# Key stacking transfers of items 19 to 23 issued by ScalarE instead of SyncE, in a four-layer attention, expert and depth-routing kernel

## The reference

```python
x = x + L0_xattn(layernorm(x), ctx, mask)    # cross attention, self attention, gelu FFN, 16 heads of 16
x = x + L0_ffn(layernorm(x))                 # 7 experts + no-op, top 2 of 8, capacity 256
x = x + L1_xattn(layernorm(x), ctx, ctx)     # cross attention, 16 heads of 16
x = x + L1_ffn(layernorm(x))                 # upper half of the tokens by score through a gelu FFN
# attention: softmax(q k^T / 4) v, then a projection
```

## Time and profile before

| | us |
|---|---|
| median of 3 runs | 857.49 |
| lowest and highest of them | 852.05, 859.93 |
| the profiled execution | 855.1 |
| its span, first to last instruction | 853.1 |
| mean granted TensorE clock | 0.929 |

### The profile page before, as it was taken

The page is one execution under the profiler, slowest core; times in us unless marked ns, Lnnn a source line. Parts: engine busy times, 40 slices in busy tenths (PEclk is TensorE's granted clock), DMA queues, the critical chain, the costliest instruction groups (busy, mean ns, idle before and its releaser), DMA issues.

```text
span 853.1 us, 18296 instructions
## 1 busy us (share of the span) xinstructions
PE 729.4 (85%) x7218; PEld 607.8 (71%) x7218; DVE 648.7 (76%) x1250; ACT 455.6 (53%) x695; POOL 409.2 (48%) x395
## 2 busy tenths in 40 slices
PE   5788999999999778999894599993677889888897
PEld 4666777777777546999883599992455657656897
DVE  7768888888888653799887377756876889877864
ACT  4256777777777566656432144421145557667342
POOL 7874654534665454624466241107577236473400
PEclk9979999999999899999995699996769989999999
DMA  6687786679776602000030577634586637500011
GB/s 190 131 136 119 140 125 99 104 118 140 115 107 102 88 3 99 26 1 22 24 128 11 154 235 245 194 68 110 86 148 95 98 60 106 85 2 2 13 39 49
DMA packets 57065, 81.47 MB, mean 95 GB/s; under 512 B 8434, under 2 KB 35057, under 8 KB 56932
## 3 DMA queue, kind: packets, MB, share of 16 engines
q1 hardware_dynamic: 53730, 74.11, 45.1%
q0 software_dynamic: 3072, 6.04, 2.9%
q10 hardware_dynamic: 178, 0.16, 0.1%
HBM read 36.74 MB, written 10.11 MB: 55 GB/s over the span
## 4 chain that ended last, share of the span: by engine, by line
PE 61%; DVE 19%; issue 7%; DMA 4%; ACT 4%; POOL 2%; SPq 1%; another core or an unknown queue 0%; ACTq 0%; DVEq 0%; POOLq 0%
PE ps L216 13%; PE ps L218 11%; PE ps L217 11%; PE ps L785 7%; PE ps L853 7%; DVE nmax L1623 6%; PE ps L807 5%; ACT prob L1151 2%; PE ps L827 2%; DMA kst<-k_parts 2%; POOL gat L1469 1%; PE ps L240 1%; PE ps L249 1%; SPq L568 1%; DMA gat<-moe_out,slu 1%
## 5 line engine op out<-in xcount | busy, mean ns | idle before, releaser
L1623 DVE TENSOR_REDUCE nmax<-ps 128x4 f32<-128x1024 f32 x192 | 234.3, 1223 | 69.8 <-PE ps L785 65.0
L1151 ACT ACTIVATE prob<-ps 128x1024 f32<-128x1024 f32 x192 | 196.4, 1023 | 70.4 <-PE ps L807 64.5
L1380 POOL TENSOR_TENSOR rstd<-var,half 128x2 f32<-128x2 f32 x56 | 43.9, 785 | 243.7 <-DVE var L1550 173.0
L785 PE MATMUL ps<-kst,qst 50*128 50x256 f32 (+1 forms) x768 | 99.6, 339 | 34.0 <-DVE nmax L1623 27.3
L853 PE MATMUL ps<-prob,vext 128*32 128x256 f32 x1536 | 107.0, 398 | 1.2 <-ACT oext L1164 1.2
L785 PEld LDWEIGHTS ps<-kst,qst 50*128 50x128 f32 (+1 forms) x768 | 60.9, 196 | 66.0 <-DVE nmax L1623 44.8
L807 PE MATMUL ps<-qst,kst 51*128 51x256 f32 (+1 forms) x768 | 83.3, 296 | 14.6 <-ACT prob L1151 13.8
L807 PEld LDWEIGHTS ps<-qst,kst 51*128 51x128 f32 (+1 forms) x768 | 61.6, 194 | 21.4 <-ACT prob L1151 17.1
L853 PEld LDWEIGHTS ps<-prob,vext 128*32 128x32 f32 x1536 | 41.2, 112 | 33.2 <-issue 4.1
L1164 ACT ACTIVATE oext<-ps 128x256 f32<-128x256 f32 x96 | 36.9, 385 | 31.7 <-PE ps L827 17.4
L1388 POOL TENSOR_SCALAR hres<-xres,mv,rstd 128x256 f32<-128x256 f32 x42 | 52.1, 1246 | 2.2
(11 more groups left out here) (287 smaller groups left out, 2315.3 us busy)
## 6 DMA issues: line engine op xcount, KB each, us to landing
kst<-k_parts SPq DMA_DIRECT2D x138, 128.0 KB, 5.1
qst<-q_parts SPq DMA_DIRECT2D x132, 128.0 KB, 3.8
e_raw<-in_ein SPq DMA_DIRECT2D x7, 1024.0 KB, 5.2
e_raw<-in_eout SPq DMA_DIRECT2D x7, 1024.0 KB, 6.1
ctx_raw<-in_ctxT SPq DMA_DIRECT2D x16, 256.0 KB, 5.5
out<-xres SPq DMA_DIRECT2D x8, 256.0 KB, 2.2
moe_in<-zeros SPq DMA_DIRECT2D x14, 128.0 KB
moe_out<-vext SPq DMA_DIRECT2D x7, 256.0 KB, 5.9
```

The source lines that it names most:

```text
L785: last = pe.matmul(score_pair(n, p)[:, 512 * s + S * t:512 * s + S * (t + 1)], qst[j][a:b, p, t * P:(t + 1) * P], kst[j][a:b, p, :], start ...
L1151: act.activation(probs[p % 4][:].rearrange("p i t s -> p (i t s)"), T_PS, ACT.Exp).then_inc(sm["exp_done"], 1)
L1380: last = gp.tensor_tensor(rstd[i][:], var[i][:], half[:], ALU.pow)
L1623: dve.tensor_reduce(nmax[n % 2][:, :, :, p].rearrange("p t s -> p s t"), score_pair(n, p).rearrange("p (s t k) -> p s t k", s=2, t=TB), AX ...
```

## The change

The six key transfers of items 19 to 23 leave SyncE's stream. A new generator `stack_k` on ScalarE issues them, with the same source, target, semaphore and the same two conditions (`st_ps` of the set's last user, `k_split` of the item). `ACT_ORDER` puts each right behind the item's `values` step. Items 1 to 18 stay as they were.

```diff
             "queries 21.1": "attention 17.13", "high 21.0": "attention 18.10", "queries 22.0": "values 21.0",
+            "stack_k 0.0": "values 19.0", "stack_k 1.0": "values 20.0", "stack_k 2.0": "values 21.0", "stack_k 3.0": "values 22.0", "stack_k 4.0": "values 23.0",
...
-                             *(stack_mask(n) for n in range(B + 4)), *(stack_k(n) for n in ITEMS if n), *(stack_q(n) for n in ITEMS),
+                             *(stack_mask(n) for n in range(B + 4)), *(stack_k(n) for n in ITEMS if n and n < NA + 3), *(stack_q(n) for n in ITEMS),
...
+                def stack_k(n):
+                    j = SET[n]
+                    yield start_of(n) - 6.7
+                    act.wait_ge(sm["st_ps"], HG * (last_user(n) + 1))
+                    act.wait_ge(sm["k_split"], n + 1)
+                    for s in range(2):
+                        for c in range(3):
+                            act.dma_start(kst[j][64 * s + DH * c:64 * s + DH * (c + 1), :, :].bitcast(F32),
+                                          PARTS["k"][c][64 * s:64 * s + 64, :, :].bitcast(F32)).then_inc(sm[f"stk_k{j}"], 16)
...
-... *(values(n) for n in ITEMS), *(attention(n) for n in ITEMS),
+... *(values(n) for n in ITEMS), *(stack_k(n) for n in ITEMS if n >= NA + 3), *(attention(n) for n in ITEMS),
```

More of the change, by code:

```diff
@@ L1269, in mod @@
                                            ACT.Copy).then_inc(sm["hid_hi"], 1)
-                side_by_side(ACT_ORDER, setup(), mask_rows(), stack_rows(0, "k", -10.05), stack_rows(0, "q", -8.9), stack_rows(NA, "q", T_C0 - 8.9), *(queries(n) for n in ITEMS), *(high(n, "k", kv_start(n) - 8.1 if n else -14.5) for n in ITEMS), *(values(n) for n in ITEMS), *(attention(n) for n in ITEMS),
+                side_by_side(ACT_ORDER, setup(), mask_rows(), stack_rows(0, "k", -10.05), stack_rows(0, "q", -8.9), stack_rows(NA, "q", T_C0 - 8.9), *(queries(n) for n in ITEMS), *(high(n, "k", kv_start(n) - 8.1 if n else -14.5) for n in ITEMS), *(values(n) for n in ITEMS), *(stack_k(n) for n in ITEMS if n >= NA + 3), *(attention(n) for n in ITEMS),
                              *(ffn(f) for f in range(B)), *(route(g) for g in range(len(GROUPS))), *(expert(e) for e in range(NE)), *(expert_weights(e) for e in range(NE)),
```

## The result

| | before | after |
|---|---|---|
| median | 858.71 us (852.05 to 860.08, 4 runs) | 875.69 us (869.58 to 876.89, 4 runs) |
| profiled execution | 855.1 | 876.4 |
| its span | 853.1 | 874.4 |
| granted clock, whole span | 0.929 | 0.913 |

The ratio is 1.0194, with a 95% interval from 1.0150 to 1.0238: slower by 17 us. The forecast was 866.5, from 857 to 874, so the median lies 1.7 us above the range, and the loss is nearly twice the 9.0 us of the sum. Of the three outcomes the one that came, slower by over 1%, had 0.48.

A forecast was written before the change was run, and what follows sets the result against it. The prediction took TensorE, with 61% of the chain, to bound the kernel, with no idle time to absorb ScalarE's delays. Its terms, 2.7 + 0.5 + 3.1 + 2.3 + 0.4 = 9.0 us, on 857.5 gave 866.5 us, range 857 to 874.

The forecast's parts named there:

- the sum: Delays forecast for items 19 to 23 added up: 2.7 + 0.5 + 3.1 + 2.3 + 0.4 = 9.0 us.
- rival 1: New waits at items 19, 21 and 22 each also cost a clock fall of 1.7 us: 871.6 us; chance 0.18.
- The bound and the mechanism: TensorE holds 61% of the chain; ScalarE's issues delay the next activation, and TensorE has no idle time to absorb it.
- The run-ahead: ScalarE's sequencer runs ahead of its engine, so a series starts when the last waiting instruction ahead of it starts.
- The price of a series: Six key issues on ScalarE hold it 3.75 us, about 0.6 us each, as on SyncE.
- Item 19: Issues delay the oext copy, the L827 transposes wait 3.3 us, and TensorE is 2.7 us late.
- Item 20: Issues may start ahead of the values copy's end; between 0.1 and 1.6 us late, taken as 0.5.
- Items 21 and 22: Held exponentials delay L807 by 2.6 (3.6) and 2.15 (2.5) us, taken as 3.1 and 2.3.
- Item 23: L807 is 2.4 us (3.8) late, mostly covered by the 1.93 us key wait; taken as 0.4.
- Rival 2: Issues are cheap or hidden on ScalarE, 0.33 us each, costing 2.6 us in all: 860.1 us; chance 0.22.
- Rival 3: Holds under 0.7 us per place vanish; item 23's key wait and clock fall go: 853.9 us, faster; chance 0.10.
- Rival 4: VectorE's own work absorbs the delays of items 19 and 20, 3.2 us less: 863.3; chance 0.50 together with the forecast.

The follow-up runs named there:

- small: Kernel before, all keys on SyncE, plus six small ScalarE transfers in series at each of five places: 876.88 us, ratio 1.0200.
- small_spread: Kernel before plus 30 small ScalarE transfers, placed one by one behind the values copy and five exponentials per place: 861.00 us, ratio 1.0021.
- lump19_20: Kernel before with only the keys of items 19 and 20 issued in series by ScalarE: 861.02 us, ratio 1.0035.
- lump23: Kernel before with only item 23's six keys issued in series by ScalarE: 863.00 us, ratio 1.0028.
- lump21_22: Kernel before with only the keys of items 21 and 22 issued in series by ScalarE: 869.06 us, ratio 1.0119.
- warm_key_b: Second run of the kernel before with 16 extra unused matmuls ahead of item 23's score pass: 855.96 us, ratio 0.9982.
- warm_key: Kernel before with 16 extra unused matmuls on TensorE ahead of item 23's score pass: 857.75 us, ratio 0.9982.
- spread23: Kernel before with only item 23's keys on ScalarE, issued one or two at a time behind running activations: 862.36 us, ratio 1.0026.
- warm: Changed kernel plus unused TensorE matmuls ahead of the waiting L808 at items 21, 22 and 23: 871.94 us, ratio 1.0137 to the kernel before.
- again: The changed kernel run a second time, unaltered: 876.42 us, ratio 1.0220 to the kernel before.
- half: Kernel before with three of six key transfers per item 19 to 23 issued by ScalarE, three by SyncE: 864.14 us, ratio 1.0046.

## Why the prediction was wrong, point by point

**What failed, in short.** Two steps. The sum put nothing for the granted clock behind the new waits, which rival 1 had priced: it cost 1.5 and 1.4 us at items 21 and 22, and an untested part of item 19. And at item 23 the sum took the whole wait of 1.93 us for the keys as cover, where only 0.90 us were free.

**The bound and the mechanism: right.** The issues hold ScalarE, the exponential behind them is late, and TensorE has no idle time in which that could vanish. Run small shows that the hold alone is enough, and small_spread that the same issues without the hold cost little or nothing. The run-ahead ("only once the last semaphore wait is over") was right to a tenth: at item 21 the first issue starts 0.14 us behind the start of the values copy.

**The price of a series: a little low.** The forecast took 3.75 us; from first issue to last the five lasted 4.10, 4.68, 3.79, 3.96 and 4.66 us. The long ones have an issue of 1.5 us or more in them.

**Item 19: 2.7, measured 4.4** by the traces (by the times of run lump19_20 together with item 20 3.0 or less, with an interval that holds both). L828 waited 3.57 us where 3.3 were forecast. Behind it the clock was at half for ten microseconds, which was not in the term; how the 4.4 split into hold and clock was not tested. Untouched kernels lose clock there too in some traces: where it was 1.00 from values copy to values copy the kernel before, lump23 and lump21_22 needed 24.90 to 25.12 us (and warm_key_b 23.11), where it was 0.87 and 0.94 warm_key needed 25.90 and spread23 26.95.

**Item 20: 0.5, measured 0.6** by the traces: the exponential was 3.39 us late, and TensorE had other work for most of that.

**Items 21 and 22: 3.1 and 2.3, measured 4.2 and 4.0.** The holds were 2.7 and 2.6 (run warm), near the terms; the clock added 1.5 and 1.4. In run lump21_22 item 22 cost 5.2, with a longer stretch at half clock. Rival 1 had this with 1.7 each, and its argument against itself (TensorE is nearly fully busy ahead of the places) did not count: the clock fell all the same.

**Item 23: 0.4, measured 2.7** (by the times of run lump23, and by the trace of the changed kernel; again has 1.4 and lump23's trace 4.9). This is the step that failed in its logic and not in a size: "These waited 1.93 us anyway and the keys land no earlier, so only 0.1 (1.35) is left." The figure is not what its own premise gives: 2.4 (3.8) less 1.93 is 0.5 (1.9), and the working from there to 0.1 (1.35) is not given. The keys were indeed no earlier. But a wait for several semaphores is put down to the one that came last. In the kernel before, the maximum that the score pass also waits for was ready at 744.43, only 0.90 us ahead of the start at 745.33:

```profile
743.20 1.23 DVE L1623 TENSOR_REDUCE nmax<-ps 128x4 f32<-128x1024 f32 x1 [0.60 <-PE ps L785]
```

A delay of TensorE delays this maximum too, so the cover was 0.90 and not 1.93. The changed kernel's 1.18 us ended by nmax are that other wait, laid bare. The pass starts 4.27 us later (12.75 us behind the values copy in place of 8.48). TensorE's two waits there, 3.31 and 0.69, less 0.90, make 3.1 of it; the 1.2 us that are left I put down to the clock, which was 0.50 behind them, without a test of it. The 1.5 us of clock that the kernel before lost behind the wait for the keys come off again, which gives 2.8 against the trace of before and 2.7 against the mean of the three untouched ones.

**The sum.** 4.4 + 0.6 + 4.2 + 4.0 + 2.7 = 15.9, where 16.0 to 17.0 were measured and 9.0 forecast. Of the 6.9 that were missing 1.7 are item 19, 2.8 items 21 and 22 (2.9 of clock, less 0.1, as the waits themselves came out 2.7 + 2.6 against 3.1 + 2.3), 2.3 item 23 and 0.1 item 20. The close fit owes something to chance, as single traces differ by more than a microsecond at items 19, 22 and 23.

**The rivals.** Rival 1 gave 871.6, from three falls, with 0.18. It had the right cause at items 21 and 22, close in size; it still lacked item 23. Rival 2 fell: an issue lasted 0.62 us in the median, not 0.33. Rival 3 fell twice over: the holds were far above 0.7 us, and run spread23 shows keys and queries side by side landing later, not sooner. Rival 4, that the delays of items 19 and 20 are absorbed, does not fit the traces at item 19 (29.36 to 29.98 us where no untouched trace is above 26.95); the times of run lump19_20 alone do not exclude it.

**The page on issuing engines.** The Trainium skill, page "DMA: Bandwidth & Descriptors", section "Issuing engines are not separate DMA queues", says that starting DMAs on several engines saves only the sequencer's time, as all run on the same 16 DMA engines. That no bandwidth is gained held: with a second queue run spread23 had 123 GB/s at item 23 where the kernel before had 136.

## What to carry to other kernels

On ScalarE an issue cost little or nothing beside an activation that was already running (run small_spread), and held what stood behind it for its 0.6 us or more otherwise; so what counts is that issues stand singly behind work that overlaps them, and that a transfer needed first is not made to share with one needed later. Before a known wait is taken as cover, look at what else that wait covers: only the time between the second to last and the last of its conditions is free. And every one of the new long waits of TensorE in the changed kernel (2.35 to 3.57 us) was followed by half clock, while the waits of 0.5 us in run half were not. In between it went either way, as the 1.92 and the 1.32 us of the kernel before show. So expect a clock loss with each new long stall, here 1.4 to 1.5 us at items 21 and 22, and take it off where a stall goes, here 1.5 to 1.6 us at item 23; the trace has to say how long the clock stays low.

## What the runs showed of the hardware that was not expected

- Extra matmuls made a kernel faster: 871.94 against 876.42 us, with the granted clock at 1.00 behind three places where it had been 0.50 to 0.64.
- In series a ScalarE issue lasted 0.61 us in the median for 8 KB (run small) and 0.62 for 128 KB (the changed kernel), though the bytes differ by sixteen times; single ones lasted up to 1.7 us for 8 KB and up to 2.1 for 128 KB (run half), and the reason is not known.
- At item 23 two queues open at once moved the same transfers at 123 GB/s, one queue at 136, and the last key landed 1.8 us later against the values copy. At item 19 there was no such difference.
- The kernel before lost clock as well, with no wait longer than 1.32 us near: 0.50 from 688 to 692.
